# The MLP of each batch moved into the loop of hyperbolic attention, and the sums there done by accumulating DMAs

## The reference, cut to what matters

```
x = x + causal_attention(layernorm(x))      # 16 heads
x = x + mixture_of_experts(layernorm(x))
x = x + hyperbolic_attention(layernorm(x))  # 16 heads of 8 columns
x = x + relu(layernorm(x) @ w1 + b1) @ w2 + b2      # 128 -> 512 -> 128
```

## Time and profile before

| | us |
|---|---|
| three runs: median, lowest, highest | 2583.7, 2578.2, 2590.47 |
| profiled execution: span from first to last instruction | 2563.6 |
| busy over the span: PE, DVE | 2079.1 (81%), 1998.1 (78%) |
| busy over the span: ACT, POOL | 1854.7 (72%), 1663.5 (65%) |
| mean granted clock of TensorE over the span | 0.844 |

### The profile page before, as it was taken

The page is one execution under the profiler, slowest core; times in us unless marked ns, Lnnn a source line. Parts: engine busy times, 40 slices in busy tenths (PEclk is TensorE's granted clock), DMA queues, the critical chain, the costliest instruction groups (busy, mean ns, idle before and its releaser), DMA issues. The chain is left out here.

```text
span 2563.6 us, 50172 instructions
## 1 busy us (share of the span) xinstructions
PE 2079.1 (81%) x14935; PEld 1515.9 (59%) x14935; DVE 1998.1 (78%) x6007; ACT 1854.7 (72%) x3188; POOL 1663.5 (65%) x1516
## 2 busy tenths in 40 slices
PE   4999999999999979999947666666666666666599
PEld 4777777777777668888834444443433444434266
DVE  4677777777777757877768999999999999999522
ACT  2666666666666634344239999999999999999743
POOL 2767766676667400000058999999999999999600
PEclk7999999999999969999966677777777777777599
DMA  5000000000000024334200000000000000000011
GB/s 136 1 2 2 1 1 0 1 0 1 1 0 1 2 67 108 93 92 110 68 1 1 1 1 0 0 0 0 0 0 0 0 0 0 0 0 1 7 31 37
DMA packets 44067, 49.03 MB, mean 19 GB/s; under 512 B 5112, under 2 KB 27038, under 8 KB 43934
## 3 DMA queue, kind: packets, MB, share of 16 engines
q1 hardware_dynamic: 35614, 43.32, 7.0%
q10 hardware_dynamic: 8320, 4.19, 0.7%
HBM read 42.78 MB, written 4.72 MB: 19 GB/s over the span
## 5 line engine op out<-in xcount | busy, mean ns | idle before, releaser
L1460 POOL TENSOR_TENSOR u<-u,spare 128x1024 f32<-128x1024 f32 x256 | 597.2, 2372 | 35.1 <-ACT spare L1433 34.9
L545 ACT ACTIVATE prob<-s_ps,nmax 128x128 f32<-128x128 f32 (+1 forms) x1024 | 364.4, 432 | 140.1 <-DVE nmax L602 140.0
L1353 PE MATMUL d_ps<-rowsT 28*128 28x256 f32 x1024 | 165.9, 404 | 331.3 <-DVE u L1532 331.2
L602 DVE CUSTOM_DVE_ANT_0 s_ps<-s_ps,mask 128x128 f32<-128x128 f32 (+1 forms) x1024 | 341.3, 385 | 101.8 <-issue 77.9
L1353 PEld LDWEIGHTS d_ps<-rowsT 28*128 28x128 f32 x1024 | 106.2, 242 | 430.4 <-issue 430.0
L582 POOL TENSOR_TENSOR g_lo<-g_all,g_hi 128x512 fp32r<-128x512 f32 x256 | 329.1, 1286 | 21.4
L1528 DVE TENSOR_SCALAR u<-d_ps 128x1024 f32<-128x1024 f32 x256 | 311.9, 1218 | 39.5 <-PE i_ps L1353 39.3
L1532 DVE SCALAR_TENSOR_TENSOR u<-i_ps,u 128x1024 f32<-128x1024 f32 x256 | 313.5, 1225 | 14.8
L1471 POOL TENSOR_TENSOR spare<-spare,u 128x1024 f32<-128x1024 f32 x128 | 303.1, 2368 | 10.7
L1447 ACT ACTIVATE u<-u 128x1024 f32<-128x1024 f32 x256 | 258.3, 1070 | 0.0
L1450 ACT ACTIVATE u<-u 128x1024 f32<-128x1024 f32 x256 | 257.5, 1066 | 0.0
(11 more groups left out here) (265 smaller groups left out, 5577.9 us busy)
## 6 DMA issues: line engine op xcount, KB each, us to landing
w_all<-w_rows SPq DMA_DIRECT2D x128, 256.0 KB, 5.6
x<-L_attn_x ACTq DMA_DIRECT2D x8, 512.0 KB, 14.0
y<-y_rows SPq DMA_DIRECT2D x16, 256.0 KB, 2.3
wkqv<-L_attn_Wkqv SPq DMA_DIRECT2D x4, 528.0 KB, 8.7
gate_rows<-L_ffn_gate_proj SPq DMA_DIRECT2D x1, 512.0 KB, 14.5
up_rows<-L_ffn_up_proj SPq DMA_DIRECT2D x1, 512.0 KB, 11.5
down_cols<-L_ffn_down_proj SPq DMA_DIRECT2D x1, 512.0 KB, 13.3
w_rows<-wT SPq DMA_DIRECT2D x8, 64.0 KB, 1.6
```

The lines of the kernel that those rows point to most:

```text
L545: last = nc.scalar.activation(prob[:, kind, at, :].rearrange("p c n -> p (c n)"), s_ps[kind][:, at.start * P:at.stop * P], ACT.Exp, bias=n ...
L602: last = nc.vector.tensor_tensor_reduce(out=scores, in0=scores, in1=keep.mask[:, N - width:N], scale=-1.0, scalar=3.4e38, op0=ALU.add, op1 ...
L1353: last = nc.tensor.matmul(ps[:, e * W2 + j * N:e * W2 + (j + 1) * N], rowsT[at, slot(i, p), 1, j * P:(j + 1) * P], rowsT[at, slot(i, p), 0 ...
L1460: nc.gpsimd.tensor_tensor(u[:, slot(i, p), :], u[:, slot(i, p), :], spare[:, p % SPARE, :], ALU.add).then_inc(sum_done, 1)
```

## The change

The MLP stage and the `rstd_of_all` ahead of it are gone. The function is now `hyperbolic_attention_and_mlp`, and its lists have these parts more, for batches behind the one at hand:

- ACT, behind all weights and the table load of Sqrt: `act_std4(b-3)`; DVE then `dve_rstd4(b-3)` at p=5 and `dve_norm4(b-3)` (two instructions) at p=6. The copy of the moments is gone.
- PE at the end of step p=2: `pe_turn_x4(b-4)`, into `r_ps[0]`. ACT, behind its first `act_hi`: `act_xT4(b-4)`, which copies it out.
- PE at the end of step p=3: `pe_hidden(b-4)`, two halves of two products each, 256 columns, into `r_ps[1]` and `r_ps[0]`. ACT, behind its second `act_hi`: `act_relu` of both halves.
- PE at the end of step p=7: `pe_y(b-4)`, ten products of 128 columns, into the second half of `o_ps`. DVE at p=0: `dve_y(b-5)` adds them to x. SP stores each batch, 128 KB, from `keep.x`.
- b1 is folded into w1 by two products at the start, b2 comes in by a product with a row of ones. So the transposing of b1 in the first stage is gone.
- The sum of ratio and root is now a DMA, issued by POOL, that adds `spare` into `u` (512 KB). Its semaphores are one for each spare. `PRODUCTS` has six pairs: two pairs more go through POOL's products, with one root on ACT and not two.
- Two rounds of three batches are written out ahead of the loop, not one, and POOL's list is written out whole. The last batches have lists of their own, with the MLP's remaining steps.

```diff
-    PRODUCTS = (0, 1, 2, 3)
+    PRODUCTS = (0, 1, 2, 3, 4, 5)
+    TURN_X4_AT, HIDDEN_AT = 2, 3
...
+        def wait_sum(engine, b, p):
+            users = 2 if p % SPARE < HP - SPARE else 1
+            after(engine, sum_landed[p % SPARE], 16 * (users * b + p // SPARE + 1))
...
+        def pe_turn_x4(pe, b, i, rows_read):
+            pe.wait_ge(xh4_done, (b + 1) * TB)
+            pe.wait_ge(rowsT_done[0], rows_read)
+            after(pe, relu_done, 2 * b)
+            for j in range(TB):
+                last = nc.tensor.transpose(r_ps[0][:, j * P:(j + 1) * P], xh4[:, i, j, :], keep.ident)
+            last.then_inc(x4_turned, 1)
+        def pe_hidden(pe, b, half, rows_read):
...
+            pe.wait_ge(xT4_done, b + 1)
...
+            for n in range(HW):
+                w = half * HW + n
+                last = nc.tensor.matmul(r_ps[1 - half][:, n * N:(n + 1) * N], w1[:, w * P:(w + 1) * P], xT4[:, :], start=True,
+                                        stop=True)
+            last.then_inc(h_ready, 1)
+        def pe_y(pe, b, copies):
+            pe.wait_ge(o_copied, copies)
+            pe.wait_ge(relu_done, 2 * (b + 1))
+            after(pe, y_done, b)
...
+        def act_std4(act, b, i):
+            act.wait_ge(var_done, (b + 1) * TB)
+            nc.scalar.activation(std4[:, i, :], part_mv[:, i, :, 1], ACT.Sqrt, bias=eps[:, 0:1]).then_inc(std4_done, 1)
+        def act_xT4(act, b):
+            act.wait_ge(x4_turned, b + 1)
+            after(act, h_ready, 2 * b)
+            nc.scalar.copy(xT4[0:P - 1, :], r_ps[0][0:P - 1, 0:N]).then_inc(xT4_done, 1)
+        def act_relu(act, b, half):
+            act.wait_ge(h_ready, 2 * b + half + 1)
+            after(act, y_ready, b)
...
         def pool_sum(pool, b, p, i):
             pool.wait_ge(root_done, b * HP + p + 1)
-            nc.gpsimd.tensor_tensor(u[:, slot(i, p), :], u[:, slot(i, p), :], spare[:, p % SPARE, :], ALU.add).then_inc(sum_done, 1)
+            nc.gpsimd.dma_start(u[:, slot(i, p), :], spare[:, p % SPARE, :], accum_op=ALU.add).then_inc(sum_landed[p % SPARE], 16)
...
+        def dve_rstd4(dve, b, i):
+            dve.wait_ge(std4_done, b + 1)
+            nc.vector.reciprocal(rstd4[:, i, :], std4[:, i, :]).then_inc(rstd4_done, 1)
...
+                        if four_before and p == TURN_X4_AT:
+                            pe_turn_x4(pe, b - 4, (i - 4) % TURN, (b + 1) * (HP // 2))
+                        if four_before and p == HIDDEN_AT:
+                            for half in range(2):
+                                pe_hidden(pe, b - 4, half, (b + 1) * (HP // 2))
+                        if four_before and p == HP - 1:
+                            pe_y(pe, b - 4, 2 * b)
...
                         if one_after and p in (0, 2):
                             act_hi(act, b + 1, p // 2)
+                        if four_before and p == 0:
+                            act_xT4(act, b - 4)
+                        if four_before and p == 2:
+                            for half in range(2):
+                                act_relu(act, b - 4, half)
                         if two_after and p == 4:
                             act_norm(act, b + 2)
+                    if three_before:
+                        act_std4(act, b - 3, i)
...
+                        if p == 0 and five_before:
+                            dve_y(dve, b - 5)
...
+                            dve_rstd4(dve, b - 3, i)
+                        if p == 6 and three_before:
+                            dve_norm4(dve, b - 3, i)
...
                             if p == 4:
+                                after(dve, relu_done, 2 * (b - 4) + 1)
                                 dve_features(dve, b + 1)
```

More of the change, by code:

```diff
@@ L1574, in turn, with written_out @@
                     known = isinstance(b, int)
-                    body(b, i, not known or b >= 1, not known or b >= 2, not known or b >= 3, not known or b + 1 < batches,
-                         not known or b + 2 < batches)
+                    before = lambda n: not known or b >= n
+                    behind = lambda n: not known or b + n < batches
+                    body(b, i, before(1), before(2), before(3), before(4), before(5), behind(1), behind(2))
             whole = batches // TURN
-            turn(0, TURN)
-            with engine.Fori(1, whole) as r:
+            for r in range(2):
+                turn(r, TURN)
+            with engine.Fori(2, whole) as r:
                 turn(r, TURN)
             turn(whole, batches % TURN)
+        def written_out(body):
+            for b in range(batches):
+                body(b, b % TURN, b >= 1, b >= 2, b >= 3, b >= 4, b >= 5, b + 1 < batches, b + 2 < batches)
         END = batches - 1
@@ L1693, in body @@
                         pool_sum(pool, b, p, i)
[L1694 removed]
+                written_out(body)
+                for p in range(HP):
+                    wait_sum(pool, END, p)
             @block.vector
@@ new lines, in _, with dve_moments @@
+                last = lambda b: b % TURN
+                def dve_moments(b):
+                    dve.wait_ge(res_done, b + 1)
+                    dve_stats(b, last(b))
+                    dve.wait_ge(stats_done, (b + 1) * TB)
+                    dve_aggregate(b, last(b))
+                dve_y(dve, END - 4)
+                dve_residual(dve, END - 2)
+                dve_moments(END - 2)
+                for j in range(TB):
+                    dve_normalise(dve, END - 1, j)
+                dve_residual(dve, END - 1)
@@ new lines, in _ @@
+                dve_moments(END - 1)
+                dve_y(dve, END - 3)
+                for n in range(2):
+                    dve_copy_o(dve, END, n, last(END))
+                for b in (END - 2, END - 1):
+                    dve_rstd4(dve, b, last(b))
+                    dve_norm4(dve, b, last(b))
+                for j in range(TB):
+                    dve_normalise(dve, END, j)
+                dve_residual(dve, END)
+                dve_moments(END)
+                dve_y(dve, END - 2)
@@ new lines, in _ @@
+                sp.dma_start(b1_row[:, :], row(io["L1_ffn_b1"])).then_inc(weights_in, 16)
+                sp.dma_start(w2[:, :, :], io["L1_ffn_w2"].rearrange("(w p) d -> p w d", p=P)).then_inc(weights_in, 16)
+                y = y_dram.rearrange("b (j p) d -> p (b j) d", p=P)
+                for b in range(batches):
+                    sp.wait_ge(y_done, b + 1)
+                    sp.dma_start(y[:, b * TB:(b + 1) * TB, :], keep.x[:, b * TB:(b + 1) * TB, :]).then_inc(y_stored, 16)
+                sp.wait_ge(y_stored, 16 * batches)
```

311 lines of the change are left out of this document (139 added, 172 removed).

## The result

The changed kernel takes 2890.9 us (median of four runs, 2886.3 to 2894.3), the kernel before 2587.1 in four runs on the same chip: ratio 1.116, 95% interval 1.113 to 1.120. Predicted were 2732 us, with 2840 as the upper end. The direction was right; of 304 us lost the prediction named 148.

What follows compares the result with a forecast made beforehand. The loop DVE - PE - DVE was taken to set 34.1 us a batch, ACT 0.8 us behind. Span 2563.6 - 110 + 258 = 2711.6 us, plus 20.1 to the runs' median: 2732 us, range 2610 to 2840.

Steps and rivals of the forecast that it cites:

- steps 1 to 5: Chain from H, the first `act_hi`'s start, through xT4 copy, hidden, ReLUs and std to DVE's 4.1 us wait in `dve_rstd4`.
- Steps 1 to 4: From H, first `act_hi`'s start: x4 ready H+4.9, hidden done H+13.6, ReLUs H+14.25, std H+24.3.
- Steps 5 and 6: DVE waits 4.1 us for std; distances of p=6 start at H+25.0, those of p=7 4.0 us later, H+29.0.
- Step 7: PE's last rows end H+34.9, `pe_y` takes 2.2 us, next distances of p=1 start H+37.7; DVE's y add hidden.
- step 2: PE's values of group 1, 1.9 us at near half clock, then hidden products: done at H+12.7 and H+13.6.
- Step 8: From distances of p=1 to the next `act_hi` 5.7 us: next H at H+43.4, so 43.3 us a batch taken.
- The first four stay at 34: The first four batches keep 34 us; only the 28 from b=4 on take 9.2 us more.
- The DMA part: Sums as DMAs, 3.7 us transfer and 1.4 fixed each: 1 us stall on ACT, covered by slack, up to 4.5 us a DMA.
- The DMAs bind: Rival: above 4.5 us a DMA the sums set the pace; at 5.5 us about 3000 us in all. Chance 0.10.
- The MLP hides: Rival: xT4 copy doesn't wait, no lag up to std, 36.3 us a batch, 2534 us. Chance 0.13.
- Half of the lag is swallowed: Rival: PE may keep full clock in values and hidden; 41 or down to 39 us a batch, 2611 to 2670. Chance 0.17.
- The tail: At the end: MLP stage's 134.1 us goes, 19 us after the last attention residual and some 5 us delay return; net -110.

Runs made afterwards that it cites:

- early_add: Changed kernel with PE's turn of x4 and hidden products moved ahead within their steps, POOL's adds for the sums and four products: 2694.8 us, ratio 1.044.
- mlp_only: Changed kernel with the sums taken back to POOL's adds and four pairs through products, MLP still in the loop: 2883.6 us, ratio 1.115.
- y_first8: `placed_dma8` with `pe_y` ahead of the values of p=4 and DVE's add of y between the two halves of the features: 2485.0 us, ratio 0.969.
- after_eight: Changed kernel with eight spare tiles instead of six: 2856.1 and 2864.1 us in two executions; two more took 3557 and 4781 us, so no ratio.
- dma_only: Kernel before, MLP kept as its own stage, with sums by accumulating DMAs and six pairs through products: 2860.5 us, ratio 1.106.
- y_first6: `y_first8` with the change's six spares instead of eight: 2753.7 us, ratio 1.074.
- placed_dma8: `placed` with the sums by accumulating DMAs, six products and eight spares: 2533.0 us, ratio 0.983.
- y_first_adds: `y_first8` with the sums by POOL's adds, four products and six spares: 2567.0 us, ratio 1.000.
- placed: Changed kernel with POOL's adds, four products; x4 turned at p=1, hidden before p=3's values, y at p=4, added at p=5, std's reciprocal at p=6: 2654.2 us.
- early_turn: Changed kernel with x4's turn right behind the pairs of p=2 and hidden ahead of the values of p=3: 2765.7 us, ratio 1.069.
- short_y: Changed kernel with only one of the four w2 products for each tile of y: 2820.8 us, ratio 1.091.

## Why the prediction missed, point by point

*The direction and its mechanism: right.* The xT4 copy behind the first `act_hi`, the hidden products late behind it, the ReLUs, std and the wait at `dve_rstd4` form one chain, as steps 1 to 5 say, and moving PE's two steps takes the lag away (`early_add` against `mlp_only`: 2694.8 against 2883.6).

*Steps 1 to 4, sizes.* With H at 2178.47: x4 ready at H+6.5 (4.9 forecast), the second ReLU done at H+16.1 (14.25), std done at H+26.0 (24.3). From there on the lengths are right to 0.3 us; nearly all of the 1.7 us arose ahead of x4. Why PE's step p=2 comes 1.6 us later behind H was not tested.

*Steps 5 and 6.* 4.02 us of waiting for std and 4.0 us from p=6 to p=7: right.

*Step 7 failed in one term, the length of `pe_y`.* It reads "then `pe_y`, 2.2 us". Measured: 5.45. The sum took 0.223 us a product from the earlier trace rows, a stretch in which PE runs without pause, at full clock. Here PE stands behind short turns with idle time between, and the clock is 0.50. Even at full clock y takes 3.0 us (1.50 a tile in `y_first8`: 0.41 for the bias row and 1.09 for four products of w2). The prediction did take the low level for the values in step 2, and not for y six steps on. Nor was DVE's add of y hidden by the wait: it is released by y itself and takes its place behind it. From the distances of p=7 to those of p=1 it is 12.7 us (2161.29 to 2174.03) where 8.7 were forecast.

*Step 8* said 5.7 us from there to the next H, and it is 4.4: ACT's gap has moved ahead of `xTs`. Together: +1.7, +4.0 and -1.3, that is 4.4 of the 4.5 us by which the settled cycle was missed (47.8 against 43.3). Over the 28 cycles, whose mean is 47.5, the miss is 120 us.

*"The first four stay at 34": wrong, a term put at nothing.* The first three cycles took 43.4 on average, and the first load came 5.6 us late: 33 us in all, shown as the ring by `after_eight` (33.8 us regained there). The DMA part followed a sum from issue to the ln that reads it, and to the roots 6 and 7 that reuse its spare. It did not follow the third user, POOL's own product 0, behind which all other products stand. By its own numbers sum 6 lands at H+52 (29.9 and six times 3.7), 9 us behind the next H, and product 0 needs that spare by then (in the settled cycle it starts at 2178.91, 0.4 us behind H). That the sums would land in under 7 us was wrong too: 11.4 in the median. So of the 154 us missed, 120 belong to the lag's cycles and 33 to the ring.

*"The DMAs bind" (0.10).* Its condition was over 4.5 us a transfer. A transfer takes 2.6 us (below) and the DMAs bind anyhow in `dma_only`, since the ring's length is the products and, behind them, seven transfers in a row. The place was wrong, not only the price.

*"The MLP hides" (0.13).* With PE's steps as they stand in the change it did not. And it couldn't have given 2534 with six spares: the ring holds any such version at 42.5 us a cycle, 2754 us in `y_first6`.

*"Half of the lag is swallowed" (0.17)* needed a PE at full clock; the mean over a cycle is 0.61.

*The tail* was right: -109.2 us against -110, and 18.4 us from the last attention residual to the end against 19 in the sum (the list of signs has 25, which doesn't fit that sum).

## What to carry to other kernels

When an engine's short instruction becomes a DMA, list every user of both its buffers and walk each one round the ring: the wait that sets the pace may be that of the issuing engine itself, and two more buffers can be worth more than the operations saved (here 8.5 us of a cycle). Price a product of TensorE at the clock of the place where it will stand, and put late small products directly behind a busy stretch, not behind the short turns at a batch's end. When two parts of a change each bring a new loop, the cycle is the longest of the loops, not their sum; test each part alone before judging either.

## What the runs showed of the hardware

- The accumulating DMA from SBUF into SBUF. With the engines' share full, two windows of the changed kernel (2168.5 to 2174 and 2174 to 2180 us) show 203 and 206 GB/s, so 512 KB take 2.6 us; loads in the first 20 us of before made 279 GB/s at a share of 0.98. The Trainium skill ("Collectives: The Full Stack", "The bandwidth ceiling") gives half of a copy's rate for an adding step of a ring of cores, which reads two sources. Against these loads, 285 GB/s at full share, the rate here is 0.71 to 0.72; a copy within SBUF was not run, so no run decides it.
- Issuing it costs POOL 0.86 us in the median and 0.97 on average, so POOL got 2.37 - 0.97 = 1.4 us a sum back. The landing took 11.4 us in the median, as five or six issued in a row queue up behind each other, and 4.6 at the least.
- Norms of 128x128 on DVE, from SBUF into SBUF, take 0.35 to 0.40 us on average in `placed_dma8`, `y_first8` and the changed kernel, 1.43 in `mlp_only`, 1.84 in `y_first_adds` and 2.17 in `placed`, beside POOL's adds. Without adds they still take 0.88 in `early_turn`, where some of them meet one of POOL's products. The price depends on where in POOL's list they fall.
- A float32 matmul of 128 columns with one row of weights isn't cheaper than one with 128 rows: 0.41 us at full clock and 0.72 at half, where four with 128 rows in a line take 0.27 and 0.50 each. It isn't the single row that makes it dearer: in `short_y`, at half clock, one product of 128 rows between two such takes 0.73 us as well. Why products are dearer there than in a line was not tested.
